# Picking each expert's first 64 tokens: every round of the search reads only the columns in which its eight can lie

## The reference, cut to what matters

```python
# x: 32 x 256 tokens of 128 channels = 8192 tokens
xn = layernorm(x)
s = two_transformer_layers(xn)                  # 2 heads of 64, 512 hidden, softmax over 256
g = silu(moe0(xn));  x = x + s * g
# moe0: 64 experts of width 96, top 8 of 64 per token, capacity C = 64
logits = xn @ router_w.T
topk_w, topk_ids = top_k(softmax(logits), 8)
pos = cumsum(onehot(flat topk_ids), axis=0)[...] - 1   # the how-manieth token of its expert
valid = pos < 64                                # only an expert's FIRST 64 tokens are computed
...
xn = layernorm(x); x = x + linear_attention(xn) * silu(moe1(xn))   # moe1: 32 experts, top 1
```

## Time and profile before

| | |
|---|---|
| median of 3 runs | 1345.54 us (1343.13 to 1346.18) |
| profiled execution, its own time | 1342.1 us |
| its span, first to last instruction | 1340.3 us, 28601 instructions |
| PE, DVE, ACT, POOL busy | 87%, 73%, 61%, 49% of the span |
| mean granted TensorE clock | 0.960 of full speed |
| block 1 ends, block 2 begins | 415.1, 415.3 us |
| block 2's first step on PE, end of block 2 | 441.3, about 822 us |

### The profile page before, as it was taken

The page is one execution under the profiler, slowest core; times in us unless marked ns, Lnnn a source line. Parts: engine busy times, 40 slices in busy tenths (PEclk is TensorE's granted clock), DMA queues, the critical chain, the costliest instruction groups (busy, mean ns, idle before and its releaser), DMA issues. The chain is left out here.

```text
span 1340.3 us, 28601 instructions
## 1 busy us (share of the span) xinstructions
PE 1165.3 (87%) x8326; PEld 933.4 (70%) x8326; DVE 978.6 (73%) x3556; ACT 818.2 (61%) x1993; POOL 652.2 (49%) x1096
## 2 busy tenths in 40 slices
PE   4999999999981799999999984988889889689993
PEld 3777778777771577777777763666667667489993
DVE  3777777777777777777777763788888888657773
ACT  2575665756651365656565652678777787557772
POOL 3443444434321254555454543265665664527775
PEclk9999999999996899999999996999999999889997
DMA  4424233242421122222222212333433433257762
GB/s 163 151 91 152 95 132 119 95 151 88 148 73 34 36 41 63 43 62 44 62 43 63 43 30 68 95 128 120 143 115 130 150 110 131 86 162 232 235 215 67
DMA packets 140732, 141.02 MB, mean 105 GB/s; under 512 B 18662, under 2 KB 119885, under 8 KB 140672
## 3 DMA queue, kind: packets, MB, share of 16 engines
q1 hardware_dynamic: 125248, 111.38, 26.1%
q0 software_dynamic: 14848, 26.77, 7.2%
q10 hardware_dynamic: 576, 2.15, 0.4%
HBM read 67.63 MB, written 62.13 MB: 97 GB/s over the span
## 5 line engine op out<-in xcount | busy, mean ns | idle before, releaser
L377 ACT ACTIVATE pr<-ps,nmx 128x256 f32<-128x256 f32 x256 | 117.9, 473 | 44.3 <-DVE nmx L424 43.7
L365 ACT ACTIVATE big<-ps,BHS 128x256 f32<-128x256 f32 x256 | 107.2, 470 | 60.2 <-PE ps L242 59.5
L242 PE MATMUL ps<-big,W 128*128 128x256 f32 x512 | 129.7, 398 | 5.6 <-ACT big L370 5.5
L255 PE MATMUL ps<-W,big 128*128 128x128 f32 x1024 | 130.6, 281 | 0.0
L255 PEld LDWEIGHTS ps<-W,big 128*128 128x128 f32 x1024 | 119.3, 192 | 13.8 <-ACT big L365 9.9
L2192 POOL DMA_INDIRECT out<-X,io x96 | 102.6, 1068 | 29.6 <-issue 29.6
L242 PEld LDWEIGHTS ps<-big,W 128*128 128x128 f32 x512 | 95.1, 196 | 26.6 <-ACT big L370 15.6
L424 DVE TENSOR_REDUCE nmx<-ps 128x2 f32<-128x512 f32 x128 | 82.4, 686 | 37.6 <-PE ps L277 37.1
L1003 POOL DMA_INDIRECT ffn<-big,si x64 | 93.8, 1466 | 26.4 <-issue 26.4
L432 DVE COPY pT<-ps 128x512 f32<-128x512 f32 x128 | 82.6, 686 | 9.2 <-PE ps L286 8.7
L510 POOL TENSOR_TENSOR big<-big,EPS 128x2 f32<-128x2 f32 x32 | 6.7, 210 | 154.1 <-DVE big L459 154.1
(11 more groups left out here) (287 smaller groups left out, 3319.1 us busy)
## 6 DMA issues: line engine op xcount, KB each, us to landing
srt<-big SPq DMA_DIRECT2D x16, 1584.0 KB, 5.7
X<-srt SPq DMA_DIRECT2D x24, 800.0 KB
big<-we SPq DMA_DIRECT2D x16, 768.0 KB, 7.3
big<-we SPq DMA_DIRECT2D x16, 384.0 KB, 3.4
X<-srt SPq DMA_DIRECT2D x24, 256.0 KB
big<-x SPq DMA_DIRECT2D x32, 128.0 KB, 2.2
X<-big SPq DMA_DIRECT2D x32, 128.0 KB, 2.1
xw<-big SPq DMA_DIRECT2D x32, 128.0 KB, 1.9
```

The costliest lines, as they stand in the source:

```text
L242: last = pe.matmul(pb[2 * g + f // 2][:, f % 2 * S:(f % 2 + 1) * S], W0[:, l, 512 + f * P:512 + (f + 1) * P], zT2[:, g, :], start=True, st ...
L255: last = pe.matmul(pb[4 + g][:, t * C:(t + 1) * C], hT[:, g, f, t * P:(t + 1) * P], W0[:, l, 1024 + f * C:1024 + (f + 1) * C], start=(f == ...
L365: act.activation(hT[:, g, f, :], pb[2 * g + half][:, f % 2 * S:(f % 2 + 1) * S], ACT.Silu, bias=BHS[:, l, f:f + 1], scale=GELU).then_inc(s ...
L377: last = act.activation(pr[:, g, h, t, :], pb[2 * g + h][:, t * S:(t + 1) * S], ACT.Exp, bias=nmx[:, g, h * TPU + t:h * TPU + t + 1], accu ...
```

## The change

Each round of `largest` now takes its own slice of the source. `full` is the whole range. With `per=None` (`pick_words`) round r reads from column 8r to the end: the 8r keys already found are non-empty words in order, so the next ones cannot stand in the first 8r columns. With `per=4` (`pick_tokens`) round r reads columns 8r to 32(r+1): each of the 64 entries of the list was cut into four pieces of which at least one is non-empty, so the first 8(r+1) non-empty pieces lie in the first 8(r+1) entries, 32(r+1) columns.

```diff
-        def largest(dve, src, least):
+        def largest(dve, full, least, per=None):
             for r in range(CAP // 8):
+                src = full[:, 8 * r:8 * per * (r + 1)] if per else full[:, 8 * r:]
                 dve.max(out=lst[:, 8 * r:8 * r + 8], in_=src)
                 dve.drain()
                 if r < CAP // 8 - 1:
                     dve.match_replace(out=src, in_to_replace=lst[:, 8 * r:8 * r + 8], in_values=src,
                                       imm_value=least)
                     dve.drain()
...
-            largest(dve, work[:, 0:4 * CAP], 0.0)
+            largest(dve, work[:, 0:4 * CAP], 0.0, 4)
             split(dve, 1, 4.0, 1, False)
-            largest(dve, work[:, 0:4 * CAP], 0.0)
+            largest(dve, work[:, 0:4 * CAP], 0.0, 4)
```

## The result

The changed kernel takes **1339.30 us** (median of 6 runs, 1337.49 to 1340.69), the kernel before 1344.41 (6 runs, 1343.13 to 1346.18). The ratio is 0.9961, 95% interval 0.9950 to 0.9971: 5.1 us less, where 4.97 was forecast. The forecast time of 1340.6 lies 1.3 us above the measured one, of which 1.1 us is that the median of before itself came out lower with six runs than with three. A later set of runs of the same two kernels gives 1340.19 us (8 runs) against 1343.78 (18 runs), ratio 0.9971, 95% interval 0.9958 to 0.9983: 3.6 us less. Both sets show a gain; neither measures it to better than about 1.5 us.

The account below looks back on a forecast made before the run. DVE's search was taken as the path at block 1's end and block 2's head; 0.41 us in pick_words plus 4.56 in pick_tokens, 4.97 us, off 1345.54 gave 1340.6 us, range 1338.0 to 1343.5.

Parts of the forecast that it names:

- The sum: Narrower max and match_replace save 0.41 us in pick_words and 4.56 in two searches of pick_tokens, 4.97 us together.
- The bounds for widths below 64: For 32 and 56 columns in pick_tokens: sum 4.80 us if nothing got cheaper below 64, 5.3 if 32 columns fell furthest.
- On the path: At block 1's end and block 2's head the other engines wait for DVE's search, so its whole saving reaches the end.
- Nothing late next: Other inputs of block 2's first step have over 16 us of slack against the 4.56 us taken away.
- The gaps: The 0.07 to 0.08 us of nothing behind each drained search instruction stays and does not grow.
- instruction-stream rival: Shorter instructions expose one more gap in each search of block 2, losing 0.9 us: 1341.5 us; chance 0.04.
- The clock: In block 2 PE's clock rises 4.0 us after PE resumes, as before; bounds 1.3 us gained or 2.9 us lost.
- The rival of price per instruction: Search instructions on DVE are charged by the piece, not by column, so nearly no gain: 1345.5 us; chance 0.04.
- What would show it: Profile signs: max of 32 columns about 0.18 us, round 0 to copy 13.5 us, block 2 behind firsts unchanged.
- off the path: Another input takes over at block 2's head, leaving 0.41 us (1345.1), or waits return half (1343.1); chance 0.09.

Follow-up runs that it names:

- tokens-only run: The changed kernel with narrowed ranges in pick_tokens alone, pick_words reading 512 columns in every round; 1337.94 us against 1343.45, ratio 0.9963.
- again: The changed kernel itself, nothing altered, profiled in a later set of runs; 1340.19 us, ratio 0.9971.
- eight-column kernel: The changed kernel with every round of pick_tokens reading only 8 columns, so later rounds miss tokens; 1347.70 us against 1343.78, ratio 1.0030.

## Why the prediction was right

- **The sum.** 0.41 + 4.56 us was forecast and 0.40 + 4.57 us of instruction time went. The agreement to 0.01 us is partly luck: in the two searches `max` gave 2.35 us (2.43 forecast) and `match_replace` 2.22 (2.14), and the two errors cancelled. Each width lay within 10 ns of the line through 64, 256 and 512 columns. The bounds for widths below 64 were not needed: `max` of 32 columns took 181 ns (176 by the line).
- **On the path.** The step from idle partners to "the search is the path" held, and in both directions: -4.45 us and +7.90 us in the stretch to `firsts`. PE's wait came to 13.04 us (12.9 forecast), POOL's to 14.24 (14.1).
- **Nothing late next.** Correct: none of the inputs with 16 us of slack appeared, even with another 4.3 us taken away.
- **The gaps.** "They stay, and do not grow" was wrong for one of 45: the gap in round 5 grew from 0.14 to 0.27 us. That is the mechanism of the instruction-stream rival, at 0.13 us and not 0.9, and it accounts for the 4.45 us (4.57 less 0.13 is 4.44).
- **The clock** is the weak step. I took the same delay and a term of zero, and named a rise more than 5 us behind PE's resumption as a sign of being wrong. It rose 5.9 us behind it in the first profile of the changed kernel, so by that sign the assumption failed there; the cost was only 0.24 us. In the second profile it rose after 4.0 us, at no cost. What I did not have is that it can fall once more in the first step, for 2.2 us. The forecast came out because these terms are small beside the range, not because the clock was understood.
- **The rival of price per instruction** fell by the widths in the profile and by the tokens-only run.
- **What would show it:** block 2's length behind `firsts` was to be unchanged and is 0.9 us longer after (382.9 us against 382.0) and 1.2 in "again"; blocks 2 to 4 did seem to take back 3 us in the first pair of profiles. For block 3 the time at 0.50 goes with it; for block 2 it stays open whether up to about 1 us is really given back, which is the milder form of the rival "off the path".
- **The closeness of the total** (5.1 us against 4.97) is luck to within about 1.5 us: the second set gave 3.6, and the tokens-only kernel 5.5 with less narrowing.

## What to carry to other kernels

Where one engine works and all others wait for it, the sum of its instruction times is the forecast for that stretch: count columns, take the price from the widths that the trace already has, and check who is idle. Then look at that engine's own waits ahead of the serial part, in program order. Here they were worth as much (4.3 us) as the narrowing, for three moved lines. When single profiles differ by less than the blocks behind the edit scatter, compare the stretch with the edit in it, and ask the granted clock about the rest before calling it noise.

## What the runs showed of the hardware

- DVE's `max` took 160, 181, 211, 260, 360 and 686 ns for 8, 32, 56, 104, 200 and 512 columns, `match_replace` 143, 168, 192, 243 and 670 ns for 8, 32, 56, 104 and 512: by these ends a fixed part of about 0.15 and 0.135 us and 1.04 us per thousand columns. The 128-partition rows of 64 columns lie within 10 ns of it. The Trainium skill (VectorE: DVE Perf Modes, The TRN2 errata) gives about 150 cycles as the measured fixed term, and (N+151)/0.96 ns for an fp32 `tensor_tensor` addition of N columns. Carried over to `max`, as an estimate, this would be 691 ns for 512 columns and 166 for 8; the trace has 686 and 160.
- A gap without a releaser sat at a fixed place of DVE's code and moved when 24 instructions were put ahead of it, 0.14 to 0.46 us long.
- With 64 filler transposes the clock was at 1.00 from 432.5 us to 442.7 and at 0.50 for the scores, PE having stood still from 439.0 to 442.0. With 16 it was at 1.00 from 428.6 to 435.4 and back at 0.50 before PE resumed at 436.2. A filler ahead of one wait did not help what stands behind the next.
- The same work of PE (10.2 of 13.5 us busy at 1.00) was followed by a fall of the clock to 0.50 for 6.8 us in one execution and by none in another, for 2.2 us. Block 3 took 348.4 to 351.3 us with 24 to 37 us of it at 0.50.
- 30 gathers of the same size landed in 3.5 us and not 2.7 when the lists of rows were others (eight-column kernel).
